# Two spread tensor-tensor instructions for each unit's norm on GpSimd, and new instruction orders, in a two-layer scan and expert network

## The reference

```python
x = x + conv(ln(x))          # ln(v) = (v - mean(v)) / sqrt(var(v) + eps) over the 64 channels
x = x + experts(ln(x))
```

## Time and profile before

| | before |
|---|---|
| median of three runs | 245.09 us |
| the profiled execution | 243.74 us |
| its span in the trace | 241.9 us |
| PE busy | 208.1 us, 86% |
| DVE busy | 185.9 us, 77% |
| POOL busy | 177.5 us, 73% |
| ACT busy | 153.4 us, 63% |

### The profile page before, as it was taken

How to read it: one execution, slowest core, us unless ns; L and a number is a source line. 1 busy time by engine, 2 the same in 40 slices (tenths; PEclk the granted TensorE clock), 3 DMA queues, 4 the chain that set the end, 5 groups by cost and what they waited for, 6 DMA issues and landing times.

```text
span 241.9 us, 3831 instructions
## 1 busy us (share of the span) xinstructions
PE 208.1 (86%) x993; PEld 132.7 (55%) x993; DVE 185.9 (77%) x583; ACT 153.4 (63%) x358; POOL 177.5 (73%) x246
## 2 busy tenths in 40 slices
PE   0695787995999969999799996989969989999992
PEld 0483775784768635375463843646438338445531
DVE  2689798897689969999899879879966694435243
ACT  3593686587139756383592794589859889576440
POOL 5649989799859439975889779798894195847432
PEclk9999798999599999999999999999999999999999
DMA  3694005709604910195001940000240250052801
GB/s 105 153 223 66 1 4 143 137 29 196 129 0 109 214 34 0 48 213 97 0 0 58 210 88 1 0 0 0 79 100 0 69 111 3 0 137 42 193 26 43
DMA packets 19857, 18.52 MB, mean 77 GB/s; under 512 B 5350, under 2 KB 14716, under 8 KB 19836
## 3 DMA queue, kind: packets, MB, share of 16 engines
q1 hardware_dynamic: 19400, 18.08, 34.1%
q10 hardware_dynamic: 436, 0.20, 0.3%
HBM read 17.56 MB, written 0.72 MB: 76 GB/s over the span
## 4 chain that ended last, share of the span: by engine, by line
POOL 36%; PE 21%; DMA 17%; issue 14%; DVE 6%; ACT 2%; POOLq 1%; SPq 1%; DVEq 0%; ACTq 0%
DMA gates_b<-gates_dram 13%; POOL total L664 10%; PE bank L1263 8%; POOL norm_a L599 6%; POOL norm_e L599 6%; PE bank L1148 5%; PE bank L1149 4%; POOL rstd_e L585 3%; POOL rstd_a L585 3%; DMA gates_dram<-gates_t 3%; PE bank L1152 2%; POOL rstd_b L585 2%; DVE weighted L1107 2%; POOL gated L631 1%; POOL fwd_h L629 1%
## 5 line engine op out<-in xcount | busy, mean ns | idle before, releaser
L1148 PE MATMUL bank<-tok_z,up_hi 128*128 128x512 f32 (+1 forms) x224 | 86.5, 393 | 2.9 <-DVE tok_z L973 1.6
L1149 PE MATMUL bank<-tok_z,up_lo 128*128 128x512 f32 (+1 forms) x224 | 81.5, 370 | 0.0
L1263 PE MATMUL bank<-hidden,down 128*64 128x512 f32 (+1 forms) x288 | 61.8, 566 | 0.0
L664 POOL TENSOR_TENSOR total<-total,weighted 128x512 f32<-128x512 f32 (+1 forms) x47 | 52.6, 1120 | 12.0 <-DVE weighted L1110 7.9
L818 ACT ACTIVATE silu_h<-bank 128x512 f32<-128x512 f32 (+1 forms) x80 | 39.9, 513 | 33.4 <-PE bank L1149 28.9
L1148 PEld LDWEIGHTS bank<-tok_z,up_hi 128*128 128x128 f32 x224 | 44.2, 197 | 22.4 <-issue 9.6
L836 ACT ACTIVATE hidden<-bank,expert_bias 128x512 f32<-128x512 f32 x64 | 39.9, 694 | 13.5 <-PE bank L1149 11.2
L1149 PEld LDWEIGHTS bank<-tok_z,up_lo 128*128 128x128 f32 x224 | 44.1, 197 | 5.9
L1088 DVE TENSOR_TENSOR hidden<-silu_h,bank 128x512 f32<-128x512 f32 (+1 forms) x80 | 43.7, 569 | 1.3 <-PE bank L1149 0.4
L1263 PEld LDWEIGHTS bank<-hidden,down 128*64 128x64 f32 x288 | 19.0, 140 | 29.3 <-issue 23.0
L1107 DVE TENSOR_TENSOR weighted<-bank,gates_b 128x512 f32<-128x512 f32 (+1 forms) x35 | 19.5, 575 | 1.3 <-PE bank L1263 1.1
(11 more groups left out here) (119 smaller groups left out, 357.0 us busy)
## 6 DMA issues: line engine op xcount, KB each, us to landing
gates_b<-gates_dram SPq DMA_DIRECT2D x12, 512.0 KB, 6.3
gates_b<-gates_dram SPq DMA_DIRECT2D x6, 1024.0 KB, 9.8
up_raw<-in_L_ffn_w_dram SPq DMA_DIRECT2D x8, 192.0 KB, 4.5
up_raw<-in_L_ffn_W_dram SPq DMA_DIRECT2D x2, 512.0 KB, 10.8
up_raw<-in_L_ffn_w_dram SPq DMA_DIRECT2D x4, 128.0 KB, 2.8
down<-in_L_ffn_w_dram SPq DMA_DIRECT2D x1, 512.0 KB, 7.6
down<-in_L_ffn_W_dram SPq DMA_DIRECT2D x1, 512.0 KB, 7.2
out_dram<-rows SPq DMA_DIRECT2D x4, 128.0 KB, 1.8
```

The lines of the kernel that those rows point to most:

```text
L664: nc.gpsimd.tensor_tensor(t, t, weighted[:, n % WEIGHTED, 0:c], ALU.add).then_inc(s_sum, 1)
L1148: nc.tensor.matmul(dst, hi, z, start=True, stop=False)
L1149: return nc.tensor.matmul(dst, lo, z, start=False, stop=True)
L1263: last = nc.tensor.matmul(t[k * D:(k + 1) * D, 0:c], w, hidden_of(first + k, j), start=(j == 0), stop=(j == l))
```

## The change

The norm of a unit on POOL becomes two instructions, whatever the number of tiles: rows minus mean, over all tiles at once with the mean spread along the 64 channels, then, in place, times rstd spread in the same way. Between them POOL waits for its own first instruction (link). The semaphore s_norm becomes one for each engine that could take a share, with a helper wait_norm; since every entry of NORM_BY is still P, POOL makes all norms as before, and the waits stay the same in effect. rstd, statistics and everything behind the norm stay as they were.

```diff
-                    for i in range(tiles_of(u)):
-                        last = nc.gpsimd.tensor_scalar(norm[n][:, i, :], row_tile(u, i), moments[n][:, i, 0:1],
-                                                       rstd[n][:, i:i + 1], ALU.subtract, ALU.mult)
-                    last.then_inc(s_norm[n], 1)
+                    first, end = norm_tiles(n, u, "P")
+                    i, f = first // HALF, (end - first + 1) // HALF
+                    r = unit_rows(u)[:, i:i + f, :, :] if end - first > 1 else row_tile(u, first).unsqueeze(1)
+                    t = norm[n][:, first:end, :]
+                    centred = t.rearrange("p (i f) d -> p i f d", f=HALF) if end - first > 1 else t
+                    mean = moments[n][:, first:end, 0:1].broadcast_to([P, end - first, D])
+                    if end - first > 1:
+                        mean = mean.rearrange("p (i f) d -> p i f d", f=HALF)
+                    link(nc.gpsimd.tensor_tensor(centred, r, mean, ALU.subtract))
+                    nc.gpsimd.tensor_tensor(t, t, rstd[n][:, first:end].unsqueeze(2).broadcast_to([P, end - first, D]),
+                                            ALU.mult).then_inc(s_norm[n]["P"], 1)
...
+        def wait_norm(eng, n, u, by="PSV"):
+
+            for e in NORM_BY[n][u]:
+                if e in by:
+                    eng.wait_ge(s_norm[n][e], normed(n, e).index(u) + 1)
...
 SP_ORDER = """
-gates in1 gates up1 gates gates gates gates gates gates gates store store store store
+in1 gates gates up1 gates gates gates gates gates gates store gates store store store
 """
```

More of the change, by code:

```diff
@@ L153, in normed, with norm_tiles @@
 def normed(n, engine):
-    return [u for u in range(len(UNITS)) if NORM_BY[n][u] == engine]
+    return [u for u in range(len(UNITS)) if engine in NORM_BY[n][u]]
+def norm_tiles(n, u, engine):
+    share = tiles_of(u) // len(NORM_BY[n][u])
+    first = NORM_BY[n][u].index(engine) * share
+    return first, first + share
 def by_pool_before(n):
@@ L333, in metaformer @@
         s_rstd = {n: sem(f"rstd_ready_{n}") for n in "abe"}
-        s_norm = {n: sem(f"normalised_{n}") for n in "ae"}
+        s_norm = {n: {e: sem(f"normalised_{n}_by_{e}") for e in "PSV"} for n in "ae"}
         s_turn = {n: sem(f"norm_turned_{n}") for n in "ae"}
@@ L583, in make @@
                         if u:
-                            pool.wait_ge(s_norm[n], u)
+                            wait_norm(pool, n, u - 1)
                     last = nc.gpsimd.tensor_tensor(rstd[n][:, 0:t], spread[n][:, 0:t], minus_half[:, 0:t], ALU.pow)
-                    if n != "b" and NORM_BY[n][u] == "S":
+                    if n != "b" and "S" in NORM_BY[n][u]:
                         link(last)
@@ L703, in make @@
                         act.wait_ge(s_turn[n], u)
-                    for i in range(tiles_of(u)):
+                    for i in range(*norm_tiles(n, u, "S")):
                         last = nc.scalar.activation(norm[n][:, i, :], row_tile(u, i), ACT.Identity,
                                                     bias=shift[n][:, i:i + 1], scale=rstd[n][:, i:i + 1])
-                    last.then_inc(s_norm[n], 1)
+                    last.then_inc(s_norm[n]["S"], 1)
                 return make
@@ L933, in make @@
                     dve.wait_ge(s_stats[n], u + 1)
-                    if u and NORM_BY[n][u - 1] != "S":
-                        dve.wait_ge(s_norm[n], u)
+                    if u:
+                        wait_norm(dve, n, u - 1, "PV")
                     for k in range(tiles_of(u)):
@@ L958, in make @@
                         dve.wait_ge(s_turn[n], u)
-                    for i in range(tiles_of(u)):
+                    for i in range(*norm_tiles(n, u, "V")):
                         last = nc.vector.tensor_scalar(norm[n][:, i, :], row_tile(u, i), moments[n][:, i, 0:1],
                                                        rstd[n][:, i:i + 1], ALU.subtract, ALU.mult)
-                    last.then_inc(s_norm[n], 1)
+                    last.then_inc(s_norm[n]["V"], 1)
                 return make
```

98 lines of the change are left out of this document (49 added, 49 removed).

## The result

The changed kernel took 231.56 us in the median (230.85 to 231.96); the kernel before, run beside it on the same chip, 244.82 (241.66 to 245.18). The ratio is 0.948, 95% interval 0.940 to 0.957. The prediction of 241.4 us, with a range from 236.6 to 247.0, had the sign right and less than a third of the size: 13 us went, not 3.65. The profiled execution took 231.47 us, its span 229.7, as against 243.74 and 241.9.

A forecast was written before the change was run, and what follows sets the result against it. No engine is full; a path across engines sets the end, POOL's latencies counting most (36% of the chain). Layer 1 -3.2, middle -1.45, start +1.0 sum to -3.65: 245.09 becomes 241.4 us, range 236.6 to 247.0.

The forecast's parts named there:

- The price of a norm: POOL's norms: 0.73 us per 128x256 instruction, a four-tile norm 1.54 instead of 2.27 us; 10.9 us leave POOL.
- the bounds: POOL's new 128x256 norm instruction: 0.41 us from below, 1.13 from above, where nothing is saved.
- the start: Unit 0 up to the first expert product: new order costs 0 to 2.2 us, 1.0 taken; product at about 26.3.
- the middle: Layer 0's experts, 40 to 160 us: four norm_e waits, at most 2.9 us, halved to 1.45 for DVE's little idle time.
- ceiling: Whole chain of waits: eleven four-tile and three two-tile norms at full saving, 8.5 us.
- layer 1: From 160 us: five PE waits for norms, four winning 0.73 and the fifth 0.3, sum 3.2 us.
- rival 1: Whole kernel: the whole chain is shortened by 8.5 us and PE keeps its clock; 236.6 us, chance 0.15.
- Rival 3: Start decides: first expert product later than about 27, PE at 1.2 GHz, DVE never makes it up; 247.3 us, chance 0.21.
- Rival 2: No change: middle gains 0, start costs 2.2, gelus on ACT eat a third of layer 1's gain; 245.2 us, chance 0.17.
- rival 4: POOL's new norm instructions no cheaper, 1.13 us each; only the start's 1.0 is left, 246.1 us, chance 0.04.
- The forecast's own range: Whole kernel: 239.5 to 243.8 us, from middle 0 to 2.9 and start 0 to 2.2; chance 0.43.
- Signs that were named: Profile after: 36 norm instructions, 0.70 to 0.76 us for 128x256, POOL near 166.6, PE's norm waits about 14 us.

The follow-up runs named there:

- experiment 10: Changed kernel plus ten single, linked POOL instructions at its end (plain and spread operands, tensor_scalar with memory or constant scalars), results unread; 236.52 us including them.
- experiment 2: Changed kernel with the five order strings of before, keeping the new two-instruction norm; 233.45 us, ratio 0.955 to the kernel before.
- Experiment 4: Old orders, only the nine norms ahead of the conv blocks (norm_a) in the new form, norm_e as before; 237.42 us, ratio 0.982 to the kernel before.
- experiments 7 and 8: Old orders, new norm, plus an unread POOL power on 128x4 per four-tile norm: behind it 239.57 us (0.987), ahead of it 245.02 us (1.001).
- experiment 6: Kernel before with five more pairs of unread PE products ahead of unit 2's transpose, to keep the clock; 244.98 us, ratio 1.006.
- experiment 1: Changed kernel with its new order strings but the old norm, one tensor_scalar per tile on POOL; 238.46 us, ratio 0.974 to the kernel before.

## Why the prediction fell short

- **The price of a norm: right in kind, off in size.** It took 0.73 for each instruction and measured 0.62. The reason is the innermost spread (experiment 10). The row of pick times shares in the earlier trace rows did spread in this way, 0.408 for 128x128 where a spread over tiles took 0.45, and the prediction quoted both but chose the 128x256 rows, which spread over tiles. The saving was 0.97 instead of 0.73, and POOL lost 15.4 us, not 10.9. The measured 0.62 lies within the bounds.
- **What of it lies on the path: this is the step that failed.** Up to unit 5's transpose the sum had +1.0 for the start and -1.45 for the middle, -0.45 together. The traces have -8.5 there, and so nearly all that is missing. The prediction had counted eleven four-tile and three two-tile norms in the chain of waits for its ceiling, and then summed only nine, those for which PE's list showed a wait in the middle (four) and in layer 1 (five). Apart from the program's first norm, these five of the chain have no term in the sum (start, us, norm in the chain of the kernel before; the fourth tile of the last two follows by itself):

```profile
9.40 1.19 POOL norm_a L599 x2
...
20.95 1.15 POOL norm_e L599 x2
24.03 2.68 POOL norm_a L599 x4
...
94.22 1.45 POOL norm_a L599 x3
...
122.89 1.50 POOL norm_a L599 x3
```

- For the first three PE waited too, 1.25, 1.14 and 1.26 us, but the start's term left them out, and by 40 us experiment 2 was 2.9 us ahead. For the last two no transpose waited. Experiment 4 shows that norm_a counts beyond PE's list, and experiments 7 and 8 show how the cost splits: a norm that no transpose waits for still delays what is queued behind it on POOL.
- The middle was then halved because "DVE has only 120 - 107.2 = 12.8 us of idle time". That was four times the 2.9 us at stake, and so no reason. DVE's idle time did shrink with the gain, busy 107.2 of 120 before, 110.6 in experiment 2 and 115.8 in the changed kernel, and was never used up. From 40 us to unit 5 experiment 2 gained 4.5 us in place of 1.45; the four waits at the measured saving are 3.9, halved 1.9.
- For the norms in the old orders, the chain of waits had the better account. By line, the kernel before shows:

```profile
DMA gates_b<-gates_dram 13%; POOL total L664 10%; PE bank L1263 8%; POOL norm_a L599 6%; POOL norm_e L599 6%; PE bank L1148 5%; PE bank L1149 4%; POOL rstd_e L585 3%; POOL rstd_a L585 3%; DMA gates_dram<-gates_t 3%; PE bank L1152 2%; POOL rstd_b L585 2%; DVE weighted L1107 2%; POOL gated L631 1%; POOL fwd_h L629 1%
```

- Norms are 6 + 6% of 241.9 us there, 29 us. A norm shrinks from 2.27 to 1.30, by 43%: 12.4 us, and experiment 2 measured 4.5%, 11 to 12 us. The prediction's own ceiling, 11 x 0.97 + 3 x 0.27 = 11.5 us with the measured savings, says the same (0.27 is a two-tile norm, 1.15 before and two of 0.40 with a wait of 0.08 now). So for the norms the first half of rival 1, the whole chain shortened, was the mechanism, with the price too low; its second half, the clock, goes with some 2 us of 13 by the executions named in experiment 6. But the chain gives a ceiling, and it is not always reached. With the new orders and the old norm (experiment 1) the chain by line shows:

```profile
POOL total L677 13%; PE bank L1276 8%; POOL norm_e L612 8%; POOL norm_a L612 6%; PE bank L1161 6%; PE bank L1162 5%; POOL gated L644 4%; POOL rstd_e L598 3%; POOL up_lo L629 3%; POOL fwd_h L642 3%; POOL gated L636 3%; POOL rstd_b L598 3%; POOL rstd_a L598 2%; PE bank L1165 2%; POOL pick L654 1%
```

- 14% of 236.4 us times 43% would be 14 us there, and the new norm brought 6.9 (238.46 to 231.56). With the norms shortened another path, through PE (61% of the chain after), ends last.
- **Layer 1: about right.** From unit 5's transpose to the end the gain was 3.7 us (8.5 to 12.2), forecast 3.2. In the old orders it was 4.4 (7.4 to 11.8).
- **The start: later than forecast, and regained.** The gating of unit 0 was expected about 1 us later and came 1.85 later, at 16.72 for 14.87; the scans behind it stood waiting for ACT twice. DVE's residual came at 22.20 for 18.45, and the first expert product 6.05 us later, not 2.2. Yet unit 2 was ahead by 55.73. In experiment 1, where the norm gives nothing, the first product is 7.3 us late and unit 2's transpose still comes at 58.44 for 59.11. So the start's term has the wrong sign. Of the 2.6% that the orders gain alone, little comes at the start, 0.7 us by unit 2, and 4.1 by unit 5 (146.63 for 150.73). That it is the work put ahead of unit 0 that pays this back is argued from the order, not shown by a run of its own.
- **The rivals.** Rival 3's trigger came (a first product beyond 27, and a granted clock of 0.51 from 24 to 30 us) and its consequence did not; "DVE, full from there to 160, never makes it up" is refuted by unit 2's row. Rival 2's zero in the middle is refuted by experiment 2, rival 4's 1.13 us by the 0.62. The Trainium skill's rule that the prediction weighed (GPSIMD Engine Reference, section 4.1 Engine selection) says that two-input instructions run about twice as slow on this engine as on VectorE, and one-input ones roughly at line rate. On two inputs the traces come near it: a 128x256 sum of two plain tiles took 0.72 us on POOL and 0.42 on DVE (at 23.60 in the changed kernel). On one input they do not: tensor_scalar with constants took 1.07 us for the same 256 columns. So rival 4, which took the rule for a choice between two forms on POOL, did not come. The forecast's own range, with its terms for middle and start, comes to 239.0 to 244.1 and not 239.5 to 243.8; nothing hangs on it.
- **Signs that were named.** 36 instructions came for 64, the waits of PE went further down than the 14 us named (to 9.1), 128x256 and POOL's 162.1 came out below their bands, and 128x128 at 0.40 just below 0.41. DVE's spread instructions grew, see below.

What stays open is which of the moves in the orders bring the 2.6% that they bring with the old norm: only SP's were tried apart. No version tried beats the changed kernel by more than a run's scatter.

## What to carry to other kernels

Where work runs round a loop through several engines, take a faster step's share of the chain of waits, times the fraction saved, for the ceiling, and don't cut it down to the list of one engine's waits, which leaves out every step that is late only through something else. Here the ceiling was reached in the old orders and half reached in the new ones; a filler as long as the saving, put back ahead of the step, tells which. An engine that is 90% busy is no reason for a discount as long as its idle time is several times the gain at stake. And a faster instruction and a better order that both attack one wait are worth less together than apart: measure each alone before adding them.

## What the hardware showed beyond that

- On POOL one tensor_tensor over 256 columns (0.72, or 0.61 with an innermost spread) is faster than one tensor_scalar over the same (1.07, or 1.22 with scalars from memory). A power on 128x4 takes 1.01 to 1.03 us, as long as 1.6 of the new 128x256 instructions.
- Some instructions of DVE and POOL that run side by side are longer than alone. DVE's spread_a of four numbers takes 0.42 us on the mean of seven, 0.27 before, with one of 1.16 among them, which ended at 46.12 as POOL's up_lo did at 46.10. At 23.59 POOL's multiplication took 0.90 instead of 0.61 beside DVE's sum of scans, and DVE's next sum, from 24.05, took 0.89, against 0.59 for unit 0's at 14.96. Seven spreads at 0.15 are about 1.0 us in all; whether any of it reaches the end was not tried.
